# Spreading four slot rounds over the routing steps, and one gate and up chunk ahead of the phase boundary

## The chip, the cores and the metric

One core of one Trainium2 chip runs the whole program. The metric is the device time of one execution in microseconds (us); less is better. The engines are TensorE (PE, with its weight loads as PEld), VectorE (DVE), ScalarE (ACT), GpSimd (POOL) and SyncE (SP), whose queue issues most DMAs.

## The reference, cut to what matters

A cross attention (16 batches of 100 tokens, width 256, context of 361) is followed by a soft mixture of 16 experts with 64 slots each. The change touches only the second part:

```python
x = _layernorm(x, norm_g, norm_b)
logits = einsum('bnd,esd->bnes', x, se)
dispatch = softmax(logits, axis=1)                     # over the tokens
combine = softmax(logits over all e*s, axis=-1)        # over the slots
slots = einsum('bnd,bnes->besd', x, dispatch)
gate = gelu(einsum('besd,edf->besf', slots, Wg) + bg)
up = einsum('besd,edf->besf', slots, Wu) + bu
eout = einsum('besf,efo->beso', gate * up, Wd) + bd
out = einsum('bns,bso->bno', combine, eout)
```

## The kernel before, in words

Three phases follow one another: attention, routing, experts. Each is a block of five instruction streams, one for each engine, and all engines meet at a block's end.

**Routing** is a software pipeline over the 16 batches. In step t, batch t+2 is normalised (DVE, with POOL for the inverse roots), batch t+1 gets its logits, batch t its exponentials, and batch t-1 its weights. Steps -2 to 2 and 12 to 17 are written out; 3 to 11 are a hardware loop. The names in a step:
- TensorE: `rt_x` (transposes of the normalised rows), `rt_logits`, `rt_lT` (transposed logits), `rt_out` from `e_comb` (combine transposes, two groups of four) and `rt_out` from `disp_n` (dispatch transposes, eight). Both kinds of `rt_out` share two banks, so the combine transposes wait until DVE has copied `dispT` out of them, and the dispatch transposes until ACT has copied `combT`.
- ACT: `l_sb`, `combT`, `xn`, `rt_xnT`, `e_comb` and eight `e_disp` exponentials.
- DVE: `neg_max`, `neg_max_s`, the norm (`rt_st`, `rt_y`, `rt_nx`), `rz`, `rz_slot` (needs all eight `e_disp`), `dispT`.
- POOL: `disp_n` (needs `rz_slot`), two short operations for each of the two norms.
- SP: the store `combine<-combT` and then the store `dispatch<-dispT` of batch t-1. `combT` and `dispT` have one buffer each, so the copy of the next batch waits until the store has landed. SP issues in order: what it waits for holds back all stores behind.

**First slot rounds.** The experts need `slots = x * dispatch` for the first expert pair and the first eight batches (`disp_first[0]`, loaded back from `dispatch`). Four rounds make it: `first_slots` (four matmuls, L1286), `first_slots_hi` (ACT, fp16 high part `slot_h`, L1294) and `first_slots_lo` (DVE, the rest `slot_l`, L1302). Before the change rounds 0 and 1 stand in step 15, and 2 and 3 in step 16. SP issues the load (L1010) in step 12, behind a wait for the dispatch store of batch 10, and ahead of the combine store of batch 11.

**Experts.** The work goes by expert pair, half of the batches (h) and expert (e). For each (h, e) there are four chunks c of the hidden width: 12 matmuls on TensorE (6 gate, 6 up, L1776), GELU on ACT (`gate_sb`, L1715), a product on DVE (L1638), the high part on ACT (`hid_h`), the low part on DVE (`hid_l`); then 48 down matmuls (L1816), of which the last 30 need the `hid_l` of chunk 3. Between the chunks TensorE makes the slots of the next half (`mix`, L1749), with ACT and DVE splitting them as above. For the very first (pair 0, h = 0, e = 0), the next half's `mix` needs `disp_first[1]`, the load of batches 8 to 15 (L1536), which SP issues first thing in the phase once all dispatch stores have landed. ACT also converts the second expert's weights (`wgu_h`) after chunk 2 there.

Of the kernel before, what the change touches and what calls it, by code (L numbers as in the profile page):

```python
# [8 lines left out]
F32 = mybir.dt.float32  # L9
# [102 lines left out]
def bu_col(t, pair, e, c):  # L112
    return t[:, 1, bass.ds(2 * pair + e, 1), c]

SLOTS_RT = 6
AT_RT = {
    "lcopy": 0, "tokmax": 1, "e_comb": 2, "lT": (0, 2), "slotmax": (2, 4), "e_disp": (2, 2),
# [826 lines left out]
def routing_phase(nc, ctx, a, keep):  # L944
# [16 lines left out]
    bank_x = psum("rt_x", [P, BANK])  # L961
# [3 lines left out]
    mix_first = [psum("rt_slots", [P, BANK])[:, :], logits[:, 0, :]]  # L965
# [23 lines left out]
    def steps(eng, step):  # L989
        for t in range(-2, 3):  # L990
            step(t, t)
        with eng.Fori(3, B - 4) as b:
            step(b, 3)
        for t in range(B - 4, B + 2):
            step(t, t)
# [8 lines left out]
    @block.sync  # L1004
    def _(sp):
        def step(b, t):
            weights, exps, logit, norm = stages(t)
            if t == B - 4:
                sp.wait_ge(disp_stored, 16 * (B - 5))
                sp.dma_start(keep["disp"][:, 0:BH], dispatch_dram[0, :, 0:BH]).then_inc(keep["disp_first"][0], 16)  # L1010
            if weights:
                sp.wait_ge(combT_ready, 2 * b)
                sp.dma_start(combine_dram[:, :, bass.ds(b - 1, 1), :].rearrange("j p o n -> p j (o n)"), combT[:]).then_inc(comb_stored, 16)
                sp.wait_ge(dispT_ready, 2 * b)
                sp.dma_start(dispatch_dram[:, :, bass.ds(b - 1, 1), :].rearrange("j n o s -> n j (o s)"),
                             dispT[:].rearrange("n (j s) -> n j s", j=SC)).then_inc(disp_stored, 16)

        steps(sp, step)
# [41 lines left out]
    def _(dve):  # L1060
        def part(s, b, t):
# [18 lines left out]
            for g in range(2):  # L1080
# [5 lines left out]
                if exps and s == AT_RT["slotmax"][g]:  # L1086

                    dve.wait_ge(lT_done, 2 * b + g + 1)
                    if t >= 1:
                        dve.wait_ge(edisp_ready, SC * b)  # L1090
                    nc.vector.tensor_reduce(neg_max_s[:, SG * g:SG * g + SG], lT_ps[:, g, 0:SG * N].rearrange("p (j n) -> p j n", j=SG),
                                            AX.X, ALU.max, negate=True).then_inc(slotmax_ready, 1)
            if norm and s == AT_RT["ln1"]:
# [23 lines left out]
        def step(b, t):  # L1117
# [5 lines left out]
            if t in (B - 1, B):  # L1123
                for r in range(2 * (t - B + 1), 2 * (t - B + 1) + 2):
                    first_slots_lo(nc, dve, keep, mix_first[r % 2], r)
# [4 lines left out]
    def _(act):  # L1130
        def part(s, b, t):
# [18 lines left out]
            for g in range(2):  # L1150
# [6 lines left out]
                if t == B - 1 and g == 1 and s == AT_RT["combT_out"][1]:  # L1157
                    for r in (0, 1):
                        first_slots_hi(nc, act, keep, mix_first[r], r)
# [18 lines left out]
        def step(b, t):  # L1178
# [5 lines left out]
            if t == B:  # L1184
                for r in (2, 3):
                    first_slots_hi(nc, act, keep, mix_first[r % 2], r)

        steps(act, step)

    @block.tensor  # L1190
    def _(pe):
# [42 lines left out]
        def step(b, t):  # L1234
            for s in range(SLOTS_RT):
                part(s + SLOTS_RT, b - 1, t - 1)
                part(s, b, t)
                if t == B - 1 and s == AT_RT["lT"][1]:
                    pe.wait_ge(keep["disp_first"][0], 16)
                    pe.wait_ge(xn_kept, BH)  # L1240
                    for r in (0, 1):
                        first_slots(nc, pe, keep, mix_first[r], r)
            if t == B:
                for r in (2, 3):
                    pe.wait_ge(keep["sl_ready"], r - 1)
                    first_slots(nc, pe, keep, mix_first[r % 2], r)
# [5 lines left out]
def expert_weights(nc, ctx):  # L1252
# [4 lines left out]
    def sems(name):  # L1257
# [14 lines left out]
        "slots_done": ctx.enter_context(nc.semaphore("slots_done")),  # L1272
        "sh_ready": ctx.enter_context(nc.semaphore("sh_ready")), "sl_ready": ctx.enter_context(nc.semaphore("sl_ready")),
# [8 lines left out]
def first_slots(nc, pe, keep, mix, r):  # L1282
# [4 lines left out]
    mm.then_inc(keep["slots_done"], 1)  # L1287

# [190 lines left out]
def expert_phase(nc, ctx, a, keep, out):  # L1479
# [14 lines left out]
    gate_ps = [psum(f"gate{i}", [P, ROWS]) for i in range(2)]  # L1494
    up_ps = [psum(f"up{i}", [P, ROWS]) for i in range(2)]
# [18 lines left out]
    gate_done, up_done, gelu_ready, hid_ready = sem("gate_done"), sem("up_done"), sem("gelu_ready"), sem("hid_ready")  # L1514
# [90 lines left out]
    def _(dve):  # L1605
# [18 lines left out]
        def step(pair, first, last):  # L1624
            for h in range(2):
# [3 lines left out]
                for e in range(2):  # L1629
# [4 lines left out]
                    for c in range(FC):  # L1634
# [6 lines left out]
                        if c % 2 == 0 and nxt:  # L1641
# [52 lines left out]
    def _(act):  # L1694
# [8 lines left out]
        def step(pair, first, last):  # L1703
            for h in range(2):
                hs = 2 * pair + h
                nxt = not (last and h == 1)
                for e in range(2):
                    u = 2 * hs + e
                    ex = 2 * pair + e
                    for c in range(FC):  # L1710
# [15 lines left out]
                        if c % 2 == 0 and nxt:  # L1726
                            slots_hi(hs + 1, 1 - h, 2 * e + c // 2, first and h == 0)
# [15 lines left out]
    def _(pe):  # L1743
# [15 lines left out]
        def step(pair, first, last):  # L1759
            for h in range(2):  # L1760
# [3 lines left out]
                for e in range(2):  # L1764
# [3 lines left out]
                    for c in range(FC):  # L1768
# [3 lines left out]
                        for i, (bank, done) in enumerate(((gate_ps[c % 2], gate_done), (up_ps[c % 2], up_done))):  # L1772
                            k = 0
                            for wt, st in ((wgu_h, slot_h), (wgu_h, slot_l), (wgu_l, slot_h)):
                                for kc in range(2):
                                    mm = nc.tensor.matmul(bank[:], wt[e][:, kc, i, c * P:(c + 1) * P],  # L1776
                                                          st[h][:, kc, e, :, :].rearrange("p b s -> p (b s)"), start=(k == 0), stop=(k == 5))
                                    k += 1
                            mm.then_inc(done, 1)
                        r = 2 * e + c // 2  # L1780
                        if c % 2 == 0 and nxt:
# [133 lines left out]
```

## Time and profile before

| | |
|---|---|
| median of 3 runs | 1131.01 us (1129.37 to 1132.79) |
| profiled execution | 1128.22 us, its span 1126.5 us |
| busy share of the span | PE 91%, DVE 71%, PEld 62%, ACT 53%, POOL 30% |
| mean granted TensorE clock | 0.969 of full speed |

The span is what the trace covers. Attention ends at about 353 us, routing runs from there to about 499 us, and the experts take the rest. A busy share is a mean over the phases; what a step is worth is read from the waits in its own stretch.

### The profile page before, as it was taken

To read this page: it belongs to the slowest core of one execution; us is meant where nothing else is said; L and a number is where in the kernel's file an instruction comes from. 1 tells how busy PE (TensorE), PEld (TensorE's weight loads), DVE (VectorE), ACT (ScalarE), POOL (GpSimd) and SP (SyncE) were. 2 spreads that over 40 slices of the span, in tenths; PEclk is the share of its full clock that TensorE was granted. 3 is DMA by queue.
4 is the path that set the end of the run, shared out by engine and by line. 5 is a ranking of instruction groups with operands and counts; after the bars stand their busy time and mean duration, and the time that the engine had idled before them with its cause. 6 is when DMAs were issued, how large, how long until landed. Compare 5 with 4: busy or idle time off the path is not lost.

```text
span 1126.5 us, 23121 instructions
## 1 busy us (share of the span) xinstructions
PE 1025.8 (91%) x7216; PEld 694.0 (62%) x7216; DVE 800.5 (71%) x1425; ACT 602.5 (53%) x1084; POOL 332.5 (30%) x349
## 2 busy tenths in 40 slices
PE   5688899999987888779999999999999999999996
PEld 3466777777753444455666666666666666666664
DVE  4547677777775888747777777787777777877754
ACT  2367687787853888755353434443544434444431
POOL 5258676767764543311001010010010010100000
PEclk8889999999997999989999999999999999999999
DMA  7858786867741544454235226153343261351123
GB/s 206 183 128 134 158 153 150 161 158 140 161 128 53 158 98 106 112 160 137 49 69 162 48 63 178 28 143 97 82 118 91 65 166 41 82 158 35 36 59 85
DMA packets 122125, 127.90 MB, mean 114 GB/s; under 512 B 49556, under 2 KB 110472, under 8 KB 122072
## 3 DMA queue, kind: packets, MB, share of 16 engines
q1 hardware_dynamic: 108016, 85.51, 34.3%
q0 software_dynamic: 10896, 40.61, 12.3%
q10 hardware_dynamic: 3160, 1.11, 0.6%
q8 instruction: 29, 0.48, 0.2%
q14 instruction: 24, 0.20, 0.1%
HBM read 80.22 MB, written 29.96 MB: 98 GB/s over the span
## 4 chain that ended last, share of the span: by engine, by line
PE 56%; issue 3%; DVE 3%; DMA 3%; POOL 1%; ACT 1%; DVEq 0%; POOLq 0%; ACTq 0%; SPq 0%
PE down L1816 15%; PE gate L1776 14%; PE up L1776 14%; PE mix L1756 5%; PE mix L1749 5%; PE rt_logits L1231 2%; DMA dispatch<-dispT 1%; DMA combine<-combT 1%; DVE dispT L1085 1%; ACT e_disp L1167 0%; POOL rt_rs L1047 0%; POOL rt_rs L1040 0%; DMA disp<-dispatch 0%; PE rt_out L1216 0%; DVE rt_st L1102 0%
## 5 line engine op out<-in xcount | busy, mean ns | idle before, releaser
L424 POOL TENSOR_TENSOR p_l<-p_f,p_h 121x800 f16<-121x800 f32 (+1 forms) x96 | 163.7, 1720 | 81.3 <-ACT p_h L708 80.6
L1715 ACT ACTIVATE gate_sb<-gate,bgu,un_gate 128x512 f32<-128x512 f32 x128 | 99.2, 775 | 158.9 <-PE gate L1776 158.2
L531 DVE TENSOR_REDUCE head_max<-at_rows 100x2 f32<-100x722 f32 x124 | 112.9, 910 | 73.3 <-PE at_rows L786 71.5
L1732 ACT ACTIVATE hid_h<-gate_sb,hid_scale 128x512 f16<-128x512 f32 x128 | 91.9, 718 | 101.6 <-DVE gate_sb L1638 101.6
L1816 PE MATMUL down<-wd_h,hid_h 128*128 128x256 f16 x512 | 139.4, 272 | 3.1 <-DVE hid_l L1650 2.7
L1816 PE MATMUL down<-wd_h,hid_l 128*128 128x256 f16 x512 | 139.5, 272 | 0.0
L1816 PE MATMUL down<-wd_l,hid_h 128*128 128x256 f16 x512 | 139.5, 272 | 0.0
L1638 DVE SCALAR_TENSOR_TENSOR gate_sb<-up,bu_s,gate_sb 128x512 f32<-128x512 f32 x128 | 95.8, 749 | 46.8 <-PE up L1776 44.5
L1650 DVE SCALAR_TENSOR_TENSOR hid_l<-gate_sb,hid_scale,hid_h 128x512 f16<-128x512 f32 x128 | 96.2, 752 | 23.7 <-ACT hid_h L1732 19.6
L1330 POOL DMA_DIRECT2D bd<-in_bd x16 | 8.9, 558 | 303.7 <-DVE eo L1672 303.7
L703 ACT ACTIVATE p_f<-at_cols 121x800 f32<-121x800 f32 (+1 forms) x96 | 79.7, 830 | 29.5 <-PE at_cols L808 28.5
L708 ACT ACTIVATE p_h<-p_f 121x800 f16<-121x800 f32 (+1 forms) x96 | 83.6, 871 | 3.1
L786 PE MATMUL at_rows<-kt,qt 100*100 100x362 f32 x248 | 73.2, 377 | 13.3 <-DVE head_max L531 11.3
L1776 PE MATMUL gate<-slot_h,wgu_h 128*128 128x512 f16 x256 | 76.3, 379 | 1.9 <-PEq L1877 1.9
L1776 PE MATMUL up<-slot_l,wgu_h 128*128 128x512 f16 x256 | 76.6, 381 | 0.0
L1776 PE MATMUL up<-slot_h,wgu_h 128*128 128x512 f16 x256 | 76.6, 381 | 0.0
L1776 PE MATMUL gate<-slot_h,wgu_l 128*128 128x512 f16 x256 | 76.6, 381 | 0.0
L1776 PE MATMUL up<-slot_h,wgu_l 128*128 128x512 f16 x256 | 76.4, 380 | 0.0
L1776 PE MATMUL gate<-slot_l,wgu_h 128*128 128x512 f16 x256 | 76.3, 379 | 0.0
L1672 DVE SCALAR_TENSOR_TENSOR eo<-down,un_down,bd 128x512 f32<-128x512 f32 x64 | 47.4, 749 | 39.5 <-PE down L1816 39.3
L808 PE MATMUL at_cols<-qt,kt 104*121 104x200 f32 (+1 forms) x384 | 64.4, 291 | 9.7 <-DMA qt<-max_p 7.9
L1611 DVE TENSOR_TENSOR slot_l<-mix,slot_h 128x512 f16<-128x512 f32 x60 | 41.4, 690 | 39.2 <-ACT slot_h L1701 39.2
(199 smaller groups left out, 2202.2 us busy)
## 6 DMA issues: line engine op xcount, KB each, us to landing
eo_pair<-eo SPq DMA_DIRECT2D x128, 128.0 KB, 2.4
k_parts<-kq_n SPq DMA_DIRECT2D x16, 724.0 KB, 3.7
kt<-k_parts SPq DMA_DIRECT2D x32, 362.0 KB
wgu<-in_Wg POOLq DMA_DIRECT2D x16, 512.0 KB, 4.6
wgu<-in_Wu POOLq DMA_DIRECT2D x16, 512.0 KB, 6.0
wd<-in_Wd POOLq DMA_DIRECT2D x16, 512.0 KB, 6.2
combine<-combT SPq DMA_DIRECT2D x16, 400.0 KB, 4.2
dispatch<-dispT SPq DMA_DIRECT2D x16, 400.0 KB
```

The costliest lines, as they stand in the source:

```text
L424: nc.gpsimd.tensor_tensor(p_l[i][0:kn, :, 0:N], p_f[i][0:kn], p_h[i][0:kn, :, 0:N], ALU.subtract).then_inc(p_low, 1)
L531: nc.vector.tensor_reduce(head_max[:, :, r], bank[0:N, :, 0:S], AX.X, ALU.max).then_inc(max_ready, 1)
L703: nc.scalar.activation(p_f[u][0:kn].rearrange("k (g e) n -> k g (e n)", g=2), cols_ps[0:kn, :, 0:4 * N], ACT.Exp, scale=1.0 / SCALE_INV).t ...
L708: nc.scalar.activation(p_h[u][0:kn, :, 0:N], p_f[u][0:kn], ACT.Copy).then_inc(p_hi, 1)
L786: mm = nc.tensor.matmul(bank[0:N, c, 0:SW], q[0:ROWS_A, r, N * c:N * c + N], k[0:ROWS_A, r, :], start=True, stop=True)
L808: mm = nc.tensor.matmul(cols_ps[0:kn, e // 2, (e % 2) * 2 * N:(e % 2 + 1) * 2 * N], kt[t % NBUF][0:ROWS_B, r, j * KC:j * KC + kn], qt[t % ...
L1638: nc.vector.scalar_tensor_tensor(gate[c % 2][:], up_ps[c % 2][:], keep["bu_s"][:, bass.ds(FC * ex + c, 1)], gate[c % 2][:], ALU.add, ALU.m ...
L1650: nc.vector.scalar_tensor_tensor(hid_l[:, c, :], gate[c % 2][:], keep["hid_scale"][:, bass.ds(ex, 1)], hid_h[:, c, :], ALU.mult, ALU.subtr ...
L1715: nc.scalar.activation(gate[c % 2][:], gate_ps[c % 2][:], ACT.Gelu, bias=bg_col(bgu, pair, e, c), scale=keep["un_gate"][:, bass.ds(ex, 1)] ...
L1732: nc.scalar.activation(hid_h[:, c, :], gate[c % 2][:], ACT.Copy, scale=keep["hid_scale"][:, bass.ds(ex, 1)]).then_inc(hidh_ready, 1)
L1776: mm = nc.tensor.matmul(bank[:], wt[e][:, kc, i, c * P:(c + 1) * P], st[h][:, kc, e, :, :].rearrange("p b s -> p (b s)"), start=(k == 0), ...
L1816: mm = nc.tensor.matmul(down_ps[t // 2][:, t % 2, :], ht[:, c, t * P:(t + 1) * P], wt[:, c, :], start=(c == 0 and k == 0), stop=(c == FC - ...
```

## The change

The load of the first half of `disp` moves from step 12 to step 10 of SP's stream, behind a wait for eight stores instead of eleven. The loop ends two steps earlier, so steps 10 to 17 are written out. Round r of the first slots is issued by TensorE at the end of step 11 + r, and split by ACT and DVE in step 12 + r, all in one bank that is later the first `up` bank; the bank of the norm's transposes is later the first `gate` bank. Chunk 0 of the first gate and up matmuls is issued at the end of step 15, ahead of the last batch's combine transposes. ACT loads the GELU table at the end of routing. In the first four chunks of the experts the `mix` rounds follow chunks 1 and 3 instead of 0 and 2.

```diff
+FIRST_SLOTS = B - 5
 AT_RT = {
+    "slots_lo": 3,
...
-    bank_x = psum("rt_x", [P, BANK])
+    bank_x, bank_slots = keep["gate_bank"], keep["up_bank"]
-    mix_first = [psum("rt_slots", [P, BANK])[:, :], logits[:, 0, :]]
...
-        with eng.Fori(3, B - 4) as b:
+        with eng.Fori(3, FIRST_SLOTS - 1) as b:
             step(b, 3)
-        for t in range(B - 4, B + 2):
+        for t in range(FIRST_SLOTS - 1, B + 2):
...
-            if t == B - 4:
-                sp.wait_ge(disp_stored, 16 * (B - 5))
+            if t == FIRST_SLOTS - 1:
+                sp.wait_ge(disp_stored, 16 * BH)
                 sp.dma_start(keep["disp"][:, 0:BH], dispatch_dram[0, :, 0:BH]).then_inc(keep["disp_first"][0], 16)
...
+            if s == AT_RT["slots_lo"] and 0 < t - FIRST_SLOTS <= 4:
+                first_slots_lo(nc, dve, keep, bank_slots[:, :], t - FIRST_SLOTS - 1)
...
-            if t in (B - 1, B):
-                for r in range(2 * (t - B + 1), 2 * (t - B + 1) + 2):
-                    first_slots_lo(nc, dve, keep, mix_first[r % 2], r)
...
-                if t == B - 1 and g == 1 and s == AT_RT["combT_out"][1]:
-                    for r in (0, 1):
-                        first_slots_hi(nc, act, keep, mix_first[r], r)
+                if g == 1 and s == AT_RT["combT_out"][1] and 0 < t - FIRST_SLOTS <= 4:
+                    first_slots_hi(nc, act, keep, bank_slots[:, :], t - FIRST_SLOTS - 1)
...
         steps(act, step)
+        act.wait_ge(combT_done, 2 * B)
+        gelu_table()
...
+                if s == SLOTS_RT - 1 and 0 <= t - FIRST_SLOTS < 4:
+                    r = t - FIRST_SLOTS
+                    if r == 0:
+                        pe.wait_ge(keep["disp_first"][0], 16)
+                        pe.wait_ge(xn_kept, BH)
+                    else:
+                        pe.wait_ge(keep["sl_ready"], r)
+                    first_slots(nc, pe, keep, bank_slots[:, :], r)
+                if s == SLOTS_RT - 1 and t == B - 1:
+                    pe.wait_ge(keep["sl_ready"], 4)
+                    pe.wait_ge(keep["wl_ready"][0], 1)
+                    gate_up(nc, keep, keep["gate_bank"], keep["up_bank"], 0, 0, 0)
...
+def gate_up(nc, keep, gate_bank, up_bank, e, h, c):
+
+    hi, lo, w_hi, w_lo = keep["slot_h"][h], keep["slot_l"][h], keep["wgu_h"][e], keep["wgu_l"][e]
+    for i, (bank, done) in enumerate(((gate_bank, keep["gate_done"]), (up_bank, keep["up_done"]))):
+        k = 0
+        for wt, st in ((w_hi, hi), (w_hi, lo), (w_lo, hi)):
+            for kc in range(2):
+                mm = nc.tensor.matmul(bank[:], wt[:, kc, i, c * P:(c + 1) * P], st[:, kc, e, :, :].rearrange("p b s -> p (b s)"),
+                                      start=(k == 0), stop=(k == 5))
+                k += 1
+        mm.then_inc(done, 1)
...
-                        if c % 2 == 0 and nxt:
+                        if c % 2 == (1 if first and h == 0 and e == 0 else 0) and nxt:
...
+                        if not (first and h == 0 and e == 0 and c == 0):
+                            gate_up(nc, keep, gate_ps[c % 2], up_ps[c % 2], e, h, c)
```

TensorE's queue at the end of routing, from the dispatch transposes of step 14 on. Before:

```order
L1216 MATMUL rt_out<-ident,disp_n 100x128 x8
L1202 MATMUL rt_out<-ident,e_comb 128x100 x4
L1210 MATMUL rt_lT<-ident,l_sb 128x100 x4
L1202 MATMUL rt_out<-ident,e_comb 128x100 x4
L1210 MATMUL rt_lT<-ident,l_sb 128x100 x4
L1286 MATMUL rt_slots<-disp,xn 128x128 x4
L1286 MATMUL rt_logits<-disp,xn 128x128 x4
L1216 MATMUL rt_out<-ident,disp_n 100x128 x8
L1202 MATMUL rt_out<-ident,e_comb 128x100 x8
L1216 MATMUL rt_out<-ident,disp_n 100x128 x8
L1286 MATMUL rt_slots<-disp,xn 128x128 x4
L1286 MATMUL rt_logits<-disp,xn 128x128 x4
```

The same place in the change (`up<-disp,xn` is a slot round):

```order
L1217 MATMUL rt_out<-ident,disp_n 100x128 x8
L1293 MATMUL up<-disp,xn 128x128 x4
L1203 MATMUL rt_out<-ident,e_comb 128x100 x4
L1211 MATMUL rt_lT<-ident,l_sb 128x100 x4
L1203 MATMUL rt_out<-ident,e_comb 128x100 x4
L1211 MATMUL rt_lT<-ident,l_sb 128x100 x4
L1217 MATMUL rt_out<-ident,disp_n 100x128 x8
L1304 MATMUL gate<-slot_h,wgu_h 128x512 x2
L1304 MATMUL gate<-slot_l,wgu_h 128x512 x2
L1304 MATMUL gate<-slot_h,wgu_l 128x512 x2
```

The slot round now stands between the dispatch transposes of one step and the combine transposes of the next; after step 15's dispatch transposes stands the first gate chunk, and nothing follows the last dispatch transposes.

ACT's queue in the last two routing steps and at the start of the experts. Before, from the `combT` copies of step 15:

```order
L1155 ACTIVATE combT<-rt_out 128x400 x2
L1294 ACTIVATE slot_h<-rt_slots 128x4x2x64
L1294 ACTIVATE slot_h<-rt_logits 128x4x2x64
L1148 ACTIVATE e_comb,z_tok<-l_sb,neg_max 100x1024
L1167 ACTIVATE e_disp,z_slot<-rt_lT,neg_max_s 128x100 x8
L1155 ACTIVATE combT<-rt_out 128x400 x2
L1294 ACTIVATE slot_h<-rt_slots 128x4x2x64
L1294 ACTIVATE slot_h<-rt_logits 128x4x2x64
L1877 UNCONDITIONAL_BRANCH
L1693 UNCONDITIONAL_BRANCH
L1715 ACT_TABLE_LOAD
L1715 ACTIVATE gate_sb<-gate,bgu,un_gate 128x512
```

In the change:

```order
L1155 ACTIVATE combT<-rt_out 128x400 x2
L1314 ACTIVATE slot_h<-up 128x4x2x64
L1148 ACTIVATE e_comb,z_tok<-l_sb,neg_max 100x1024
L1166 ACTIVATE e_disp,z_slot<-rt_lT,neg_max_s 128x100 x8
L1155 ACTIVATE combT<-rt_out 128x400 x2
L1185 ACT_TABLE_LOAD
L1185 ACTIVATE e_comb<-l_sb 100x1
L1890 UNCONDITIONAL_BRANCH
L1712 UNCONDITIONAL_BRANCH
L1734 ACTIVATE gate_sb<-gate,bgu,un_gate 128x512
```

One split stands ahead of step 15's exponentials instead of two, none at the end, and the table load is ahead of the phase boundary.

## Rows read from the trace of the kernel before

**Rows 1.** Chain that ended last, 455 to 525 us: start, us, what.

```profile
457.82 3.98 DMA dispatch<-dispT
...
461.81 0.33 SPq L1010
...
462.20 5.73 DMA combine<-combT
...
469.10 5.37 PE rt_logits L1231 x8
...
477.61 3.68 PE rt_logits L1231 x8
...
483.08 5.46 DMA dispatch<-dispT
...
495.63 3.95 DMA dispatch<-dispT
...
499.59 4.52 DMA disp<-dispatch
...
504.15 1.16 PE mix L1749 x8
505.31 1.30 PE gate L1776 x6
...
510.49 0.91 PE mix L1749 x8
...
511.42 0.33 ACT slot_h L1701
...
517.93 3.43 PE down L1816 x30
```

**Rows 2.** Windows from dispT copy to dispT copy: us, engines' busy, PEclk, DMA, GB/s.

```profile
448.78:456.38 7.60, 6.32 (x34) 3.74 (x34) 6.38 (x17) 6.38 (x24) 3.07 (x5) 1.00 0.46 108
456.38:463.88 7.50, 6.29 (x34) 3.74 (x34) 6.24 (x17) 6.37 (x24) 3.08 (x5) 1.00 0.34 79
463.88:474.95 11.07, 7.58 (x32) 4.08 (x33) 6.32 (x16) 6.30 (x24) 3.07 (x5) 0.85 0.49 133
...
488.62:494.06 5.44, 2.57 (x14) 2.09 (x15) 2.62 (x7) 2.62 (x13) 1.52 (x1) 0.63 0.44 114
```

**Rows 3.** Timeline of steps 12 and 13: start, us, what, [idle before <-releaser].

```profile
459.72 1.15 ACT L1148 ACTIVATE e_comb<-l_sb,neg_max 100x1024 f32<-100x1024 f32 x1 [0.35 <-DVE rz L1074]
...
460.31 0.41 DVE L1100 TENSOR_SCALAR rt_y<-x,rt_mv,rt_rs 100x256 f32<-100x256 f32 x1 [0.23 <-POOL rt_rs L1040]
...
464.71 0.53 PE L1202 MATMUL rt_out<-ident,e_comb 100*128 100x100 f32 x4 [1.13 <-DVE dispT L1085]
```

**Rows 4.** Timeline of steps 15 and 16.

```profile
484.00 1.08 PE L1286 MATMUL rt_slots<-disp,xn 100*128 100x128 f32 x8
...
485.12 0.60 ACT L1294 ACTIVATE slot_h<-rt_slots 128x512 f16<-128x512 f32 x1 [0.76 <-PE rt_slots L1286]
...
486.50 1.14 ACT L1148 ACTIVATE e_comb<-l_sb,neg_max 100x1024 f32<-100x1024 f32 x1
...
489.83 0.68 DVE L1302 TENSOR_TENSOR slot_l<-rt_slots,slot_h 128x512 f16<-128x512 f32 x1
489.87 0.39 ACT L1167 ACTIVATE e_disp<-rt_lT,neg_max_s 128x100 f32<-128x100 f32 x1
...
491.35 1.52 POOL L1031 TENSOR_TENSOR disp_n<-e_disp,rz_slot 128x800 f32<-128x800 f32 x1 [6.53 <-DVE rz_slot L1079]
```

**Rows 5.** Timeline of the experts' first chunks.

```profile
501.77 1.28 ACT L1715 ACT_TABLE_LOAD   x1 [3.48 <-PE gate L1776]
...
508.56 0.75 DVE L1638 SCALAR_TENSOR_TENSOR gate_sb<-up,bu_s,gate_sb 128x512 f32<-128x512 f32 x1
```

**Rows 6.** Tile combT, 440 to 505 us: issue to landing of its stores.

```profile
DMA to landing us min/median/max: 3.4/3.9/7.0
```

**Rows 7.** DMA queues, 483 to 488.6 us: packets, MB, share of 16 engines.

```profile
q8 instruction: 1, 0.02, 1.0%
```

More of the change, by code:

```diff
@@ L1183, in step, with gelu_table @@
                 weights_hi(nc, act, keep, 0, 0)
-            if t == B:
-                for r in (2, 3):
-                    first_slots_hi(nc, act, keep, mix_first[r % 2], r)
+        def gelu_table():
+            nc.scalar.activation(e_comb[:, 0:1], l_sb[:, 0:1], ACT.Gelu)
         steps(act, step)
+        act.wait_ge(combT_done, 2 * B)
+        gelu_table()
     @block.tensor
@@ L1237, in step @@
                 part(s, b, t)
[L1238 to L1246, printed above, removed]
+                if s == SLOTS_RT - 1 and 0 <= t - FIRST_SLOTS < 4:
[10 more added lines that the diff above has]
+                    gate_up(nc, keep, keep["gate_bank"], keep["up_bank"], 0, 0, 0)
         steps(pe, step)
@@ L1272, in expert_weights @@
         "slots_done": ctx.enter_context(nc.semaphore("slots_done")),
+        "gate_bank": ctx.enter_context(nc.psum_tensor("gate0", [P, ROWS], F32)),
+        "up_bank": ctx.enter_context(nc.psum_tensor("up0", [P, ROWS], F32)),
+        "gate_done": ctx.enter_context(nc.semaphore("gate_done")), "up_done": ctx.enter_context(nc.semaphore("up_done")),
         "sh_ready": ctx.enter_context(nc.semaphore("sh_ready")), "sl_ready": ctx.enter_context(nc.semaphore("sl_ready")),
@@ L1492, in psum @@
         return ctx.enter_context(nc.psum_tensor(name, shape, F32))
-    gate_ps = [psum(f"gate{i}", [P, ROWS]) for i in range(2)]
-    up_ps = [psum(f"up{i}", [P, ROWS]) for i in range(2)]
+    gate_ps, up_ps = [keep["gate_bank"], psum("gate1", [P, ROWS])], [keep["up_bank"], psum("up1", [P, ROWS])]
     down_ps = [psum(f"down{i}", [P, 2, D]) for i in range(2)]
@@ L1513, in expert_phase @@
     slots_done, sh_ready, sl_ready = keep["slots_done"], keep["sh_ready"], keep["sl_ready"]
-    gate_done, up_done, gelu_ready, hid_ready = sem("gate_done"), sem("up_done"), sem("gelu_ready"), sem("hid_ready")
+    gate_done, up_done, gelu_ready, hid_ready = keep["gate_done"], keep["up_done"], sem("gelu_ready"), sem("hid_ready")
     hidh_ready, hidl_ready = sem("hidh_ready"), sem("hidl_ready")
@@ L1725, in step @@
                                                  scale=keep["d_scale"][:, bass.ds(ex, 1)]).then_inc(wdh_ready[e], 1)
-                        if c % 2 == 0 and nxt:
+                        if c % 2 == (1 if first and h == 0 and e == 0 else 0) and nxt:
                             slots_hi(hs + 1, 1 - h, 2 * e + c // 2, first and h == 0)
@@ L1771, in step @@
                             pe.wait_ge(hid_ready, FC * u + c - 1)
[L1772 to L1779, printed above, removed]
+                        if not (first and h == 0 and e == 0 and c == 0):
+                            gate_up(nc, keep, gate_ps[c % 2], up_ps[c % 2], e, h, c)
                         r = 2 * e + c // 2
-                        if c % 2 == 0 and nxt:
+                        if c % 2 == (1 if first and h == 0 and e == 0 else 0) and nxt:
                             if r == 0:
```

## The prediction

> **What bounds the kernel now.** I read the chain of work that ended last first. In the experts it is TensorE, chunk after chunk, with hardly a wait, so a microsecond won before them should reach the end. The change works ahead of that, from 455 to 518 us, and there the chain is not arithmetic [rows 1]. It runs from store to store: the dispatch store of batch 10 (3.98) holds SP's load of `disp`, which holds a combine store (5.73), which holds ACT's next `combT` copy and through it the logits (5.37). Then come the dispatch stores at 483.08 (5.46) and 495.63 (3.95), the load of the second half of `disp` (4.52), and `mix` at 504.15. The last 30 down matmuls start at 517.93.
>
> The windows between two starts of the `dispT` copies give the pace [rows 2]: 7.60 in the loop, 7.50 in the written-out step 12, and 11.07 in step 13. The timeline shows how full a step is [rows 3]: ACT idles 0.35 ahead of `e_comb`, DVE 0.23 ahead of `rt_y`, TensorE 1.13 ahead of the combine transposes. All three are near their limit, and 0.6 us on an engine is not free by itself.
>
> **The load moved from step 12 to 10.** In step 12 SP waited for a store issued one step earlier. The combine store behind was ready at about 459.4, just ahead of `e_comb` at 459.72 [rows 3], and was issued at 462.20 [rows 1]. It landed at 467.93, while the transposes for the next copy were done at 464.71 + 0.53 = 465.24 [rows 3]. Of the excess of 11.07 - 7.50 = 3.57, 1.69 is the clock: the logits after the stall took 5.37, those of the next step 3.68 [rows 1], with a granted clock of 0.85 in the window [rows 2]. In step 10 the new wait, for eight stores, is met long before, so the combine store goes out when ready. Beside the load it may again take 5.73, and 459.4 + 5.73 = 465.1 is just inside 465.24. Bounds of what comes back: 3.57 (no stall) and 0 (the stall moves with the load). I take 3.57 - 0.25 = 3.3, being nearest to landing inside the step. The first round needs the load only at the end of step 11, over 10 us later.
>
> **Two more steps written out.** 7.60 - 7.50 = 0.10 each [rows 2]: 0.2 won.
>
> **The rounds in steps 12 to 15.** Each adds TensorE 1.08, ACT 0.60, DVE 0.68 [rows 4]. TensorE's stands just where it idles 1.13 for the `dispT` copy [rows 3]: nothing. ACT loses 0.60 - 0.35 = 0.25 beside DVE's loss, not on top of it. DVE's split stands ahead of `rt_y`: 0.68 - 0.23 = 0.45 at most, a little less as instruction starts overlap. What queues behind it on DVE is the second norm and then `dispT`, for which all wait. I take 0.4 in steps 12 and 13, 0.8 in all; bounds 0 and the serial sum, 2.36 a step. Step 14 has no norm and hangs on TensorE's logits, so DVE's part is covered there; step 15 comes next. So the `dispT` copies of batch 13 start 3.3 + 0.2 - 0.8 = 2.7 earlier.
>
> **Steps 15 and 16.** Their rounds are gone from these places, but the chain did not run through the last two. It hangs on the one buffer of `dispT`: copy, store, landing, copy. From the start of the copies to the store's issue is 457.82 - 456.38 = 1.44 [rows 1, 2]. The store at 483.08 goes out at 480.4; landing after 3.95 (usual) or 5.46; the next copies and store end at 485.8; landing at 489.7; the last store is issued at 491.1 in place of 495.63: 4.5 won, or 3.0 if one landing takes 5.46 again. The other branch must be earlier: ACT no longer waits 0.76 for a round, nor makes a second one, so `e_comb` moves from 486.50 to about 482.3; `e_disp` ends 490.26 - 486.50 = 3.76 later, at 486.0; `disp_n` takes 1.52 [rows 4]; so the dispatch transposes can start at about 488.0, 1.7 ahead of the landing.
>
> The chunk ahead of the last combine transposes is 2 x 1.30 = 2.6 [rows 1]. It can start near 482.9 when ACT and DVE have split round 3, and ends at 485.5, about when the `dispT` copies free the bank anyway: nothing. At half clock it is 5.2, ends at 488.1, and pushes the last dispatch transposes to 489.7 or so: at most 1 us late. The clock in this stretch was low before (0.63 [rows 2]), but with TensorE waiting; with the chunk in the wait I take full clock. The table load (1.28 [rows 5]) falls to ACT while DVE still copies `dispT`: nothing. If ACT ended last it would delay the phase boundary only, while the chain goes through the DMA.
>
> **The experts' start.** SP's load waits for the last store and takes what it took, 3.95 + 4.52. So `mix` starts 4.5 earlier, at 499.65. From `mix` to the last down matmuls it was 517.93 - 504.15 = 13.78. Of this, chunk 1 (2.6) is now done while the load is under way. The second `mix` and ACT's part of it (0.91 + 0.33 [rows 1]) leave the path to chunk 2's `hid_h`, and DVE's product (0.75 [rows 5]) takes their place: 0.5. Together 3.1 less, 10.7. Against it stands the clock. TensorE has nothing between the end of chunk 1 (495 to 497) and `mix`; after the like stall in step 13 the logits ran at half speed. I charge `mix` once more (0.9) and part of a gate chunk (0.5): 1.4. Bounds 0 and 1.7. Net 1.7.
>
> The Trainium skill (TensorE: Matmul & The Clock Gate, section on the HAM clock gate) says that the array starts at half clock after an idle stretch and is freed only by activity. Against this change that rule speaks twice, since chunk 1 and `mix` both follow a wait; by it the second term is 1.7, without it 3.1. The trace agrees with it at 469.10, where the logits after the stall ran at half speed.
>
> **Sum.** 4.5 + 1.7 = 6.2 us, on a profiled span of 1126.5 (the profiled execution took 1128.22, 2.8 below the median of 1131.01). Taken from the median: 1124.8.
>
> **Rivals.**
> - The stall moves with the load: the combine store of step 10 misses its step and the clock falls. For it: three transfers then share the engines, and DVE and ACT are as full as in step 12. Against: 2.8 of the lateness was SP's wait. Only 2.9 is won: 1128.1. Chance 0.12.
> - The rounds don't fit: 2.36 instead of 0.4 in each of steps 12 and 13, 3.9 more. For it: each step is a loop through all engines, with waits of 0.2 to 1.1. Against: the three parts belong to different steps' data and don't wait for each other. 2.3 won: 1128.7. Chance 0.08.
> - Slower: the chain is made of landings, and a landing can drag. A combine store took 7.0 where the median is 3.9 [rows 6]; an instruction fetch (q8) ran in that stretch [rows 7]. The change writes out more code just here, and so fetches more. Each such landing costs 3.1. It decides from the point where 6.2 + 3.4 = 9.6 is lost, four landings; at four the time is 1137.2. Chance 0.06. The Trainium skill (Runtime: NRT & Kernel Launch, Instruction fetch mechanics) says that the fetch ahead is mostly hidden and that taken branches are what breaks it; by this the longer code costs nothing, as the 0.10 for the written-out step suggests.
> - The forecast, with `mix` cold or warm and one slow landing or none: 3.0 + 1.7 to 4.9 + 3.1, so 1123.0 to 1126.3. Chance 0.70. The remaining 0.04 is scattered, half of it no change.
>
> **How the numbers follow.** 0.3% (3.4 us) is about what a measurement can tell from no change. The two partial cases lie just inside it, though 2.9 may measure as over: faster 0.74, same 0.20, slower 0.06. The range runs from 1121.5 (the best case, and the spread of runs) to 1128.3, which takes in the moved stall.
>
> **What would show it.** Right: no wait of over 0.5 us on a combine landing in steps 11 to 14; windows of about 7.9 in steps 12 and 13; the last dispatch store issued about 4.5 earlier, with DVE's `dispT` copies waiting for landings rather than TensorE; a TensorE wait of some 3 us ahead of the first `mix`, and about 12.1 from it to the last down matmuls. Wrong: a stall at step 11 with a low clock; windows over 9; the gate chunk at twice 2.6 with the dispatch transposes behind it; or a wait later in the experts that gives the 6 us back.

## The result and the profile after

The change is slower: 1163.2 us (median of 4 runs, 1162.3 to 1167.3) against 1130.2 for the kernel before (4 runs, 1125.5 to 1132.8), a ratio of 1.032 [1.029, 1.035]. The forecast was 1124.8 with a range up to 1128.3. The profiled execution took 1167.26 with a span of 1165.2, which is 38.7 more than before. It is the longest of its four, so the medians lie only 33.0 apart.

The page of the kernel after shows that the work is the same and its wait is not. DVE, ACT and POOL are busy as long as before within 1 us; TensorE is busy 14.8 us longer with the same number of matmuls.

```profile
span 1165.2 us, 23045 instructions
PE 1040.6 (89%) x7216; PEld 696.9 (60%) x7216; DVE 800.3 (69%) x1425; ACT 601.8 (52%) x1085; POOL 331.9 (28%) x349
...
q14 instruction: 52, 0.42, 0.2%
...
PE 51%; issue 8%; DVE 5%; POOL 2%; DMA 1%; ACT 1%; DVEq 1%; POOLq 0%; ACTq 0%
```

Two entries stand out against the page of before: "issue" has 8% of the chain (3% before), and the instruction queue q14 carried 52 packets (24 before). "Issue" is time in which an engine waits for nothing that the profile shows.

**The stretch that the change edits went nearly as forecast.** The chain of waits, the rows that answer to [rows 1]:

```profile
479.36 4.28 DMA dispatch<-dispT
...
485.05 4.13 DMA dispatch<-dispT
...
490.58 3.94 DMA dispatch<-dispT
...
494.54 4.96 DMA disp<-dispatch
...
499.54 1.23 PE mix L1768 x8
500.77 2.56 PE gate L1304 x6
503.33 1.65 PE up L1304 x6
504.98 1.31 PE gate L1304 x6
...
511.90 3.44 PE down L1829 x30
```

The last dispatch store goes out at 490.58 (495.63 before, forecast 491.1), `mix` starts at 499.54 (504.15, forecast 499.65), and the last 30 down matmuls start at 511.90 (517.93, forecast 511.75). So at 512 us the kernel is 6.0 us ahead, where the sum had 6.2. Part of this is luck. At the `dispT` copy of step 9, which both kernels still make in the same loop ahead of all that the change edits, this execution was 1.29 us ahead already. Before, and then the change:

```profile
441.18 1.28 DVE L1085 COPY dispT<-rt_out 100x512 f32<-100x512 f32 x2
439.89 1.28 DVE L1086 COPY dispT<-rt_out 100x512 f32<-100x512 f32 x2
```

The stretch itself won 6.0 - 1.3 = 4.7. Behind 512 us, 38.7 + 6.0 = 44.7 us are lost.

**The loss.** DVE's waits, grouped by line and releaser (total us, times, longest us). Before, no line of the experts' loop over pairs had a wait for "issue" of more than 0.2 us:

```profile
DVE gate_sb L1657 <- issue: 29.6, 5, 6.3
...
DVE slot_l L1630 <- issue: 12.5, 5, 2.5
```

Five and five, 42.1 us in all. DVE's part of the experts is a loop over pairs of experts that runs six times, so it jumps back five times. The timeline of DVE at one jump back:

```profile
737.85 0.17 DVE L1492 TENSOR_SCALAR d_scale<-top_down 128x2 f32 x1
743.87 0.75 DVE L1657 SCALAR_TENSOR_TENSOR gate_sb<-up,bu_s,gate_sb 128x512 f32<-128x512 f32 x1 [5.86 <-issue]
747.13 0.69 DVE L1630 TENSOR_TENSOR slot_l<-mix,slot_h 128x512 f16<-128x512 f32 x1 [2.51 <-issue]
```

`d_scale` is the last product of a pass, `gate_sb` the first of the next. The chain of waits has the instructions between them (DVEq is DVE's own branch, register and semaphore instructions), and what TensorE makes of it:

```profile
738.29 0.06 DVEq L1543
738.36 5.18 issue
743.53 0.09 DVEq L1543
...
743.87 0.08 DVE gate_sb L1657
743.95 3.11 issue
747.07 0.02 DVEq L1627
...
751.18 2.08 PE mix L1768 x8
753.25 2.56 PE gate L1304 x6
```

The branch (line 1543 is the loop) is at 738.29. The next instruction comes 5.2 us later, five go through (the chain shows four; the fifth, a register instruction of line 1661, stands in the compiled program), and then DVE stands another 3.1 us. Meanwhile TensorE uses up what it has and stops, and its clock falls: `mix` takes 2.08 where 0.89 is usual, the six gate matmuls 2.56 where 1.29 is. Its own waits add up to 26.2 us:

```profile
PE mix L1768 <- DVE x L1639: 15.3, 5, 3.7
...
PE gate L1304 <- DVE gate_sb L1657: 10.9, 5, 2.6
```

Over the five passes it is busy for 401.6 us, 384.7 before, 16.9 more for the same matmuls. Together that makes 43.1. The same can be read from the pace of the loop. This row, of the register instruction beside `d_scale`, has the time of the six passes' ends:

```profile
L1492 DVEq ALU_OP  x6: 40/40/40, 651.0 to 1079.1; - x6
```

(1079.1 - 651.0) / 5 = 85.6 us a pass. The same row of the kernel before:

```profile
L1472 DVEq ALU_OP  x6: 40/40/40, 657.1 to 1042.1; - x6
```

There a pass takes 77.0. The difference is 8.6 us a pass, 43.1 in five: nearly all of the 44.7. Another 1.7 lie behind the sixth pass, where nothing jumps back (86.1 us to the end of the span, 84.4 before); a_pad4 and b_pad48 below are slow in the loop too (84.9 and 85.1 a pass) and have 84.7 and 84.8 there, so they are not the loop's. What DVE waits for shows in the view of the DMA queues over one pass of the kernel after, 737 to 823 us (packets, MB, share of 16 engines):

```profile
q14 instruction: 5, 0.04, 0.2%
```

Five packets of 8 KB. The next pass has five again. The kernel before has 3 such packets in all of 600 to 1040 us, the kernel after 26.

### The profile page after: what moved, and what is told of

Its sections match the earlier page's. It is cut to its first block, busy times and chain, and to the rows that moved or that the text cites. A ratio compares the mean times of both kernels' runs of the same rounds, so it can differ in the third digit from the quotient of the medians.

```text
span 1165.2 us, 23045 instructions
## 1 busy us (share of the span) xinstructions
PE 1040.6 (89%) x7216; PEld 696.9 (60%) x7216; DVE 800.3 (69%) x1425; ACT 601.8 (52%) x1085; POOL 331.9 (28%) x349
## 4 chain that ended last, share of the span: by engine, by line
PE 51%; issue 8%; DVE 5%; POOL 2%; DMA 1%; ACT 1%; DVEq 1%; POOLq 0%; ACTq 0%
PE down L1829 14%; PE gate L1304 13%; PE up L1304 13%; PE mix L1775 5%; PE mix L1768 5%; PE rt_logits L1232 1%; DMA dispatch<-dispT 1%; DVE dispT L1086 1%; DVE wd_l L1677 1%; POOL rt_rs L1048 0%; DVE gate_sb L1657 0%; DMA disp<-dispatch 0%; POOL rt_rs L1041 0%; ACT e_disp L1166 0%; DVE x L1639 0%
## 5 line engine op out<-in xcount | busy, mean ns | idle before, releaser
L1768 PEld LDWEIGHTS mix<-disp,xn 100*128 100x128 f32 x480 | 65.1, 199 | 30.0 <-DVE x L1639 18.6
L1768 PE MATMUL mix<-disp,xn 100*128 100x128 f32 x480 | 66.8, 284 | 18.0 <-DVE x L1639 15.3
L1304 PE MATMUL up<-slot_h,wgu_h 128*128 128x512 f16 x256 | 80.3, 397 | 0.0
L1304 PE MATMUL gate<-slot_h,wgu_l 128*128 128x512 f16 x256 | 79.9, 395 | 0.0
L1304 PE MATMUL gate<-slot_l,wgu_h 128*128 128x512 f16 x256 | 79.3, 392 | 0.0
L1304 PE MATMUL up<-slot_l,wgu_h 128*128 128x512 f16 x256 | 79.1, 392 | 0.0
```

The lines of the kernel that those rows point to most:

```text
L1304: mm = nc.tensor.matmul(bank[:], wt[:, kc, i, c * P:(c + 1) * P], st[:, kc, e, :, :].rearrange("p b s -> p (b s)"), start=(k == 0), stop=( ...
L1768: mm = nc.tensor.matmul(mix_ps[r % 2][:, i * P:(i + 1) * P], xn_all[:, b, m * P:(m + 1) * P], disp[:, b, :], start=True, stop=True)
```

## The experiments

**The theory.** DVE's instructions come in blocks of 8 KB, 128 instructions, by that queue. In the compiled program the body of the pair loop is 262 instructions, 2 x 128 + 6, and the change puts 48 instructions more ahead of it (two more routing steps written out, and the rounds' waits). If the loop starts 1 to 5 instructions ahead of a block's end it lies in four blocks, else in three. The theory is that three blocks and the one fetched ahead stay in the engine, so that a jump back finds them, and that four don't, so that each pass fetches all again. Where the loop lies is not read from the program; the five instructions between the two stalls say that it now starts just there. **The rival**: something that the change does (its order of mixes, its first pass of the experts, its semaphores) disturbs the loop, and the packets are a symptom.

The means to tell them apart are increments of a semaphore that is not in use, on DVE, ahead of the pair loop. They compute nothing and shift the loop. The number is 5 here:

```diff
+        for _pad in range(5):
+            dve.sem_inc(waited, 1)
         pairs(dve, step)
```

**a_pad5: the change, shifted by 5.** 

> The change, with five semaphore increments more in DVE's stream ahead of the experts' first chunk; nothing else. Fetch theory: the pair loop of DVE (262 instructions, 64 bytes each) began 5 instructions before a block of 8 KB ended and so touched four blocks; now it begins on a block's edge and touches three, the jump back needs no fetch, the five waits of 6.3 and 2.5 us on DVE go, and the time falls by 5 x 8.6 = 43 us or a little more, to 1119 to 1126. Rival (the shared gate and up banks, or the moved mix rounds, slow the experts): five increments change nothing, 1163.

Measured: 1123.73 us (12 runs) beside 1127.08 for the kernel before on that chip, ratio 0.9957 [0.9936, 0.9978]. Span 1121.5, a pass takes (1036.8 - 652.0) / 5 = 77.0, and DVE has no wait for "issue" in the loop. One pass fetches no instruction packet. Five instructions that do nothing take 39.5 us off the median.

**a_pad4: the change, shifted by 4.** 

> The same with four increments, one fewer. Fetch theory: the loop still begins one instruction before the edge and touches four blocks: 1160 to 1168 as the change itself, with five long DVE waits. A theory by which the padding helps by delaying DVE, or by sheer amount, expects nearly the time of the five-increment kernel.

Measured: 1164.87 (one run). The loop now starts one instruction ahead of the block's end, so the second stall follows the first almost at once, and they appear as one of 9.0 us. The chain has one instruction between the two, where the change has five:

```profile
738.65 5.15 issue
743.80 0.09 DVEq L1543
743.89 3.48 issue
```

DVE's waits:

```profile
DVE gate_sb L1657 <- issue: 44.6, 5, 9.0
```

**b_pad48: the kernel before, shifted by 48.** None of the change is in it. 

> The kernel before, with 48 semaphore increments in DVE's stream ahead of the experts' first chunk, which puts its pair loop where the change has it (5 instructions before a block's edge). No part of the change is in it. Fetch theory: 1170 to 1178 (44 us slower), with five waits of some 6 and 2.5 us on DVE at the loop's start. Rival (banks or moved mix rounds): 1130 to 1133, 48 increments cost 2 us at most.

Measured: 1168.4 (4 runs), ratio 1.036 [1.0323, 1.0397]. It is a little under the 1170 to 1178 expected. DVE's waits are those of the change; the last row is the increments themselves:

```profile
DVE gate_sb L1638 <- issue: 29.3, 5, 5.9
...
DVE slot_l L1611 <- issue: 12.6, 5, 2.5
...
DVE top_down L1465 <- issue: 4.9, 1, 4.9
```

**b_pad47: the kernel before, shifted by 47.** 

> The same with 47 increments: the loop begins 6 instructions before the edge, and 6 + 256 = 262 just fits three blocks. Fetch theory: 1129 to 1134, as before. If the loop needs a margin behind it (a block fetched ahead that throws out the first), it is slow as the 48 one.

Measured: 1130.51 (one run), 37.9 us under b_pad48's median, with no such wait in the loop. These four settle it. Counted from the kernel before, the shifts 48 (b_pad48, and the change) and 52 (a_pad4) are slow, 47 (b_pad47) and 53 (a_pad5) are not: the five offsets that 262 = 2 x 128 + 6 asks for, wherever the shift comes from (49 to 51 were not run). The rival is dead, since the kernel before becomes as slow without a line of the change. What is shown is that the loop is fetched anew in each pass where it touches four blocks. That three and one ahead are what the engine holds is the theory's reading of it, not measured.

**a_pad128: the change, shifted by 128.** This asks for the size of the block. 

> The change with 128 increments of an unused semaphore ahead of DVE's pair loop in place of none. The increments themselves cost some 13 us once (48 of them took 4.9 in an earlier run), not all of it on the path. Theory (the loop's instructions are fetched in blocks of 128, and the loop is slow wherever it starts 1 to 5 instructions ahead of a block's end): a shift by 128 changes nothing, so DVE's waits at the jump back stay, five of about 5.9 and five of about 2.5, 42 in all, and the time is 1163 to 1180. Rival (fetched in blocks of 256 instructions, so that the loop start now lies in the middle of one): the waits are gone and the time is 1122 to 1138.

```diff
+        for _pad in range(128):
+            dve.sem_inc(waited, 1)
         pairs(dve, step)
```

Measured: 1168.49 (2 runs), ratio 1.0373 [1.033, 1.0415]:

```profile
DVE gate_sb L1657 <- issue: 29.0, 5, 5.8
...
DVE top_down L1485 <- issue: 13.2, 1, 13.2
DVE slot_l L1630 <- issue: 12.7, 5, 2.6
```

The waits repeat at a distance of 128, so blocks of 256 are out. A smaller block that divides 128 would repeat as well; that it is 128 rests on the packets of 8 KB, at 64 bytes for each instruction of the compiled program.

**b_wait8: the moved load's wait alone.** The forecast put 3.3 us on the load's move, because SP's wait for a young store held the combine store behind it. Here the load stays in step 12 and only its wait is met earlier.

```diff
-                sp.wait_ge(disp_stored, 16 * (B - 5))
+                sp.wait_ge(disp_stored, 16 * BH)
```

> The kernel before with one number changed: in step 12 SP waits for eight dispatch stores instead of eleven before it loads disp. DVE's loop stays where it was. If SP's wait made the stall of step 13, the window of step 13 falls from 11.07 to about 7.8 and the first mix starts 3.3 us earlier: 0.3% faster in time. If the stall came from the load's traffic, it stays and the time is the same.

Measured: 1124.25 (12 runs; before 1128.36 there), ratio 0.9973 [0.9955, 0.999]. The profiled execution, the longest of the twelve, has the span of before, 1126.5, a window of 11.21 where 7.8 was expected, and the stall still in it:

```profile
457.16 1.37 SPq L1013 DMA_DIRECT2D combine<-combT  x1
...
464.59 0.50 ACT L1155 ACTIVATE combT<-rt_out 128x400 f32<-128x400 f32 x1 [2.24 <-DMA combine<-combT]
...
465.67 6.71 PE L1231 MATMUL rt_logits<-seT,rt_xnT 128*100 128x512 f32 x8 [1.46 <-ACT rt_xnT L1176]
```

The combine store is issued at 457.16, 5.0 us sooner than in [rows 1]; 2.2 of that the execution was ahead at step 9 already, so 2.8 are the wait's. ACT waits for its landing until 464.59. With the load's 400 KB on the way ahead of it this combine store takes over 7 us, against a median of 3.9 [rows 6]. So SP's wait made only a part of the stall: ACT stands 2.24 us here and stood 3.44 before, 1.2 less. The logits behind take 6.71 in place of 5.37, 1.3 more, and the window comes out the same.

The times point the other way: by the ratio 3.0 us are won [1.1 to 5.1], just the 0.3% expected if SP's wait made the stall. The profiled execution had the lowest granted clock of the twelve (0.968, the others 0.970 to 0.975), so the others may have won what it lost to the clock; no trace shows it, and what the wait is worth stays open.

**a5_nochunk: a_pad5 without the chunk ahead.** It and the kernels below have the five increments.

```diff
-                if s == SLOTS_RT - 1 and t == B - 1:
-                    pe.wait_ge(keep["sl_ready"], 4)
-                    pe.wait_ge(keep["wl_ready"][0], 1)
-                    gate_up(nc, keep, keep["gate_bank"], keep["up_bank"], 0, 0, 0)
...
-                        if not (first and h == 0 and e == 0 and c == 0):
-                            gate_up(nc, keep, gate_ps[c % 2], up_ps[c % 2], e, h, c)
+                        gate_up(nc, keep, gate_ps[c % 2], up_ps[c % 2], e, h, c)
```

> The change with five increments, but chunk 0 of gate and up back at the start of the experts, not ahead of the last combine transposes. My terms: the first mix starts at the same time (it hangs on stores and load), chunks 0 and 1 both run in the wait for it (5.2 us at full clock), so nothing or up to 1 us is lost. If the chunk in the last routing step is worth its 2.6 us, mix to the last down matmuls grows by that much.

Measured: 1122.72 (8 runs), ratio 0.995 [0.9927, 0.9973], not to be told from a_pad5's. TensorE does both chunks in the wait for the load, stands only 0.32 us ahead of `mix`, and has its full clock for it and for the chunk behind:

```profile
503.36 1.16 PE L1766 MATMUL mix<-disp,xn 100*128 100x128 f32 x8 [0.32 <-DMA disp<-dispatch]
```

From `mix` to the last down matmuls it takes 514.03 - 503.36 = 10.67, where a_pad5, with the chunk done early, takes 12.35: there TensorE has run out of work, and the chunk behind `mix` runs at half clock.

**a5_mix0: a_pad5 with the mix rounds back behind chunks 0 and 2.**

```diff
-                        if c % 2 == (1 if first and h == 0 and e == 0 else 0) and nxt:
+                        if c % 2 == 0 and nxt:
```

> The change with five increments, but the first four chunks have their mix rounds after chunks 0 and 2 as before. Then chunk 1 waits behind the first mix: from mix to the last down matmuls it takes 2.6 us more, about 14 to 15 instead of 12.4, and the time is 2 to 3 us above the five-increment kernel. If the place of the rounds is worth nothing, there is no difference.

Measured: 1126.7 (12 runs), ratio 0.9976 [0.9955, 0.9997]. TensorE stands 10.99 us ahead of `mix` (a_pad5: 2.59) and starts it at half clock:

```profile
499.65 2.04 PE L1770 MATMUL mix<-disp,xn 100*128 100x128 f32 x8 [10.99 <-DMA disp<-dispatch]
```

The last down matmuls start at 515.71, 16.1 after it; in a_pad5 at 512.45, 12.4 after it. By the profiles, where the rounds stand is worth 3.3 to 3.7 us (2.6 expected). The times lean the same way, 0.9976 against a_pad5's 0.9957, but their intervals overlap.

**a5_mix23w: the rounds behind chunks 2 and 3**, and ACT's split of the second expert's weights behind chunk 1, in the same wait.

```diff
-                        r = 2 * e + c // 2
-                        if c % 2 == (1 if first and h == 0 and e == 0 else 0) and nxt:
+                        r = c - 2 if first and h == 0 and e == 0 else 2 * e + c // 2
+                        if (c >= 2 if first and h == 0 and e == 0 else c % 2 == 0) and nxt:
...
-                        if first and h == 0 and e == 0 and c == 2:
+                        if first and h == 0 and e == 0 and c == 1:
                             weights_hi(nc, act, keep, 1, 0)
```

> The change with five increments, and the idea carried on: mix rounds after chunks 2 and 3, and the second expert's weights converted on ACT after chunk 1, all in the wait for the load. From mix to the last down matmuls it should take 6 to 9 us instead of 12.4, so 3 to 6 us less than the five-increment kernel, near 1119. If ACT or DVE fall behind instead, no gain.

Measured: 1119.18 (6 runs), ratio 0.9919 [0.9893, 0.9945]. `mix` is issued 0.52 after chunk 2, at full clock behind it, and the last down matmuls follow 7.2 us later:

```profile
501.56 1.16 PE L1770 MATMUL mix<-disp,xn 100*128 100x128 f32 x8 [0.52 <-DMA disp<-dispatch]
...
508.79 0.27 PE L1831 MATMUL down<-wd_h,hid_h 128*128 128x256 f16 x1 [0.63 <-DVE hid_l L1669]
```

**a5_mix23w_b and a5_mix23w_nochunk: the same kernel again, and beside it the same without the chunk ahead**, on one chip. 

> The same kernel as a5_mix23w, beside the one without the early chunk on one chip. Expected 1117 to 1121, ratio to the kernel before 0.990 to 0.994; 1.5 to 2.5 us under a5_mix23w_nochunk by the theory, equal to it within 1 us by the rival.

> As a5_mix23w (1119.18, mix rounds after chunks 2 and 3, five increments), but chunk 0 goes back from routing to the experts. Theory (a chunk issued early is worth its own time once nothing else can fill the wait for the load): in a5_mix23w TensorE idled only 0.5 us ahead of the first mix round, so chunk 0 (1.7 to 5 us by its clock there) now stands in that chain, the first mix starts 1.5 to 2.5 us later relative to the landing, the last down matmuls are at 510.5 to 511.5 in place of 508.8, and the time is 1121 to 1122. Rival (ACT and DVE set the end of this stretch, and a busier TensorE gets its full clock earlier): no difference, 1119 within 1 us.

Measured: 1118.22 (6 runs), ratio 0.992 [0.9893, 0.9946], and without the early chunk 1121.77 (12 runs), ratio 0.9956 [0.9936, 0.9977]. The intervals just overlap; the profiles agree with the medians. In both the last `dispT` copy starts at nearly the same time, 490.14 and 490.35, and the last down matmuls start at 507.41 and 510.56. So once the wait for the load is full, the chunk is worth about 3 us, somewhat more than the 1.5 to 2.5 expected.

The kernels side by side, from their profiles. Starts in us; the step 9 copy is the last `dispT` copy that all of them make in the same loop, the last `dispT` copy is where the landings of routing end, `mix` the first round of the experts, "down" the last 30 down matmuls:

| kernel | step 9 copy | last dispT copy | mix | down | step 9 to down | span |
|---|---|---|---|---|---|---|
| before | 441.18 | 494.06 | 504.15 | 517.93 | 76.75 | 1126.5 |
| change | 439.89 | 489.27 | 499.54 | 511.90 | 72.01 | 1165.2 |
| a_pad5 | 440.40 | 489.94 | 500.10 | 512.45 | 72.05 | 1121.5 |
| a5_mix0 | 440.11 | 489.75 | 499.65 | 515.71 | 75.60 | 1124.7 |
| a5_nochunk | 442.52 | 493.41 | 503.36 | 514.03 | 71.51 | 1123.0 |
| a5_mix23w | 438.98 | 491.52 | 501.56 | 508.79 | 69.81 | 1117.8 |
| a5_mix23w_nochunk | 439.82 | 490.35 | 502.65 | 510.56 | 70.74 | 1120.7 |
| a5_mix23w_b | 440.52 | 490.14 | 500.14 | 507.41 | 66.89 | 1117.6 |

Apart from the change itself, what is won at "down" is the span's gain within 1.6 us (9.1 and 8.7 for a5_mix23w, 10.5 and 8.9 for its repeat). But the executions differ by up to 3.5 us at step 9, where the code is the same, so a single start says little; the column "step 9 to down" is free of this. What is left in it are mainly two things that differ from execution to execution: the clock of one group of logits (a5_mix23w and its repeat are the same kernel, 6.70 and 3.68 us for that group, 69.81 and 66.89 in all; a5_mix0 and a5_mix23w_nochunk have one of 5.37), and a slow landing (in a5_nochunk DVE waited 5.12 for the last but one dispatch store, where a_pad5 waited 3.81).

## Why the prediction was wrong, point by point

**The step that failed: "Two more steps written out … 0.2 won".** The instruction streams were costed by the time of a step and not by where they end up. The 48 instructions by which DVE's stream grew move the pair loop, which the change doesn't touch, to five instructions ahead of a block's end. That costs 8.6 us at each of five jumps back, 43.1 in place of a gain of 0.2. In the list of what would show it wrong stood "a wait later in the experts that gives the 6 us back", and it gave back seven times that; but no case among the rivals had it. The slower rival named the right actor, the instruction fetch, at the wrong place: a packet beside routing's landings, and four slow landings at 3.1. Of these there was none in the profile after (4.28, 4.13 and 3.94 for the last three dispatch stores). The 0.06 for "slower" was too little because longer code had been given one way to hurt, and the other was not looked for.

The Trainium skill (Runtime: NRT & Kernel Launch, Instruction fetch mechanics) says two things here. That a taken branch to a target outside the pages held forces a fetch before execution goes on: the trace agrees, 5.2 us at the branch and 3.1 at the edge behind it. And that blocks are of 256 instructions (16 KiB), two of them held: here a_pad128 repeats the stall at a shift of 128, and the packets are of 8 KB, so for DVE in this kernel the measurement decides for 128. The prediction quoted the half sentence on branches and drew from the other half that longer code costs nothing.

**The load moved: 3.3 forecast.** The size is near, the reason is not. The windows between `dispT` copies of the kernel after (columns as in [rows 2]):

```profile
447.38:455.51 8.13, 5.89 (x32) 3.59 (x33) 6.33 (x16) 5.93 (x24) 3.07 (x5) 1.00 0.50 129
455.51:463.47 7.96, 7.88 (x52) 5.55 (x51) 6.85 (x17) 7.16 (x25) 3.07 (x5) 1.00 0.40 105
463.47:471.24 7.77, 7.27 (x45) 4.78 (x44) 6.74 (x17) 6.87 (x25) 3.07 (x5) 1.00 0.43 108
...
478.04:483.73 5.69, 5.29 (x43) 4.04 (x42) 4.33 (x8) 5.19 (x17) 1.52 (x1) 1.00 0.55 132
```

The worst window is 8.13 in place of 11.07, 2.9 us less. But ACT's wait on the combine store's landing is still there, where the forecast had none of over 0.5: 2.20 us in the kernel after, 2.39 in a_pad5, 2.24 in b_wait8, against 3.44 before. So the first rival, that the stall moves with the load, was half right. The 2.9 are 1.2 of wait and 1.7 of clock: the logits behind the stall took 3.68 in the kernel after and 5.37 before. The second part is luck. The same kernel had logits of 6.70 and a window of 11.27 in a5_mix23w, and of 3.68 and 8.23 in a5_mix23w_b, behind waits of 2.34 and 2.43. So the place of the load in the program does not decide the clock; why it falls in one execution and not in the other stays open. (The 5.37 were called half speed in the prediction. They are so in part: wholly at half clock they would take 2 x 3.68 = 7.4, and the granted clock over them was 0.65, then 0.50, then 0.79.)

**The rounds in steps 12 and 13: 0.4 each.** 7.96 - 7.50 = 0.46 and 7.77 - 7.50 = 0.27. Right, and the rival of 2.36 a step is out.

**Steps 15 and 16: 4.5 from two fast landings.** The landings were 4.28, 4.13 and 3.94 and the store was issued 5.05 earlier, 3.8 without the 1.29 of before step 10. Right in its mechanism, a little too large in size. The chunk ahead of the last combine transposes ran at full clock from 482.22 to 484.99; the last `dispT` copy waited 3.83 for its landing, not for TensorE, so the chunk cost nothing, as said. What it brings was taken as 2.6 (chunk 1 moves into the wait). By a5_nochunk it brings nothing measurable: with the rounds behind chunks 1 and 3, TensorE waited 2.6 us for the load anyway, and without the early chunk both chunks fitted there, and the 1.7 us of half clock behind `mix` were not paid. It brings about 3 us only when other work fills that wait (a5_mix23w against a5_mix23w_nochunk).

**The experts' start: 12.1 from `mix` to down, 1.4 of it for the clock.** Measured 12.36. The clock's cost is right in size and not in place: `mix` itself, behind 2.71 us of idling, had a granted clock of 0.97 (1.02 us to the next start, 1.84 at half clock in a5_mix0), and the fall to 0.50 came with the gate matmuls behind it (2.56 in place of 1.3) and part of the up matmuls (1.65). Against a5_nochunk, which has the full clock there, it is 12.36 - 10.67 = 1.7, where 1.4 was charged. That 3.3 us or more came from the rounds' place and not from the chunk (a5_mix0) had not been told apart in the working.

**The sum.** Without the shifted loop the change gives 0.9957 [0.9936, 0.9978] of before, that is 2.5 to 7.2 us won, and in the profiles 5.0 by the span and 4.7 from step 9 to the last down matmuls; forecast 6.2. So it would have been inside the range, but not for all the reasons given: the load's move won partly by the clock, and the early chunk brought nothing. Of the range's bounds, the 4.9 of the best case is worked out nowhere in the prediction.

## What to carry to other kernels

When an edit makes an engine's stream longer or shorter ahead of a hardware loop, count the loop's instructions on that engine and see at how many offsets it touches one 128-instruction block more (shown here for one loop on DVE, 262 instructions, where four blocks are too many); an innocent edit elsewhere can land on such an offset. The signature is a wait for "issue" once per pass at the jump back, with instruction packets inside the loop's time where there were none; some no-op instructions ahead of the loop tell at once, and cure it. Where an engine waits for a transfer, first see how much of the work behind the transfer can be placed ahead of it: here the first `mix` two chunks later (with the second expert's weights split ahead of it; the two were not run apart) won more than the chunk done early did by itself. Work pulled out of the wait can even cost, by the idle engine's clock: the early chunk's 1.7 us. The mix rounds after chunks 2 and 3, the early chunk and the shifted loop together make 1118 to 1119, the fastest kernel of this study.

## What the runs showed of the hardware

- One instruction more or less ahead of a loop changes this kernel by about 40 us: a_pad5 against a_pad4 (1123.7 and 1164.9), b_pad47 against b_pad48 (1130.5 and 1168.4).
- A jump back to a block that is not held costs DVE 5.2 us, and the block behind it 3.1 more, with DMA engines that are busy to a share of 0.35 over the pass. Together 8.3, and the pass gets 8.6 longer. TensorE has queued work for part of the stall and stands still for 5.2 us of a pass; the other 3.4 it loses by its lower clock (16.9 us more of busy time in five passes).
- Increments of a semaphore are not free: 48 of them held DVE 4.9 us, 128 of them 13.2, about 0.1 each.
- Behind ACT's wait of 2.2 to 2.4 us for a combine landing, the logits took 6.71 in b_wait8 and 6.70 in a5_mix23w, but 3.68 in a_pad5 and in a5_mix23w_b, which is the same kernel as a5_mix23w.
- TensorE's clock can fall behind the first work after an idle stretch and not with it: in the change `mix` has 0.97 right after 2.71 us of idling, and the gate matmuls behind it 0.50.
